# Two narrow half-steps of the last query tile moved from places 12 and 13 to places 7 and 8, with three smaller moves beside them

## The reference, cut to what matters

```
std_attn = softmax(where(mask, -inf, q @ k.T * scale));  std_out = std_attn @ v
geo_attn = softmax(where(mask, -inf, lines_r @ J lines_w.T * inc));  geo_out = geo_attn @ geo_v
y = layernorm(x + ((1-gate)*std_out + gate*geo_out) @ out_w + out_b)
out = layernorm(y + (silu(y @ wg.T) * (y @ wu.T)) @ wd.T)
```

## Time and profile before

| what | value |
|---|---|
| median of 3 runs (lowest, highest) | 1618.38 us (1617.12, 1618.8) |
| the profiled execution's own time | 1618.34 us |
| its span, first to last instruction | 1616.6 us |
| mean granted TensorE clock | 0.985 |
| TensorE matmul busy | 1582.2 us, 98% |
| ScalarE busy | 1199.7 us, 74% |
| VectorE busy | 1055.6 us, 65% |
| GpSimd busy | 341.2 us, 21% |

### The profile page before, as it was taken

How to read it: one execution, slowest core, us unless ns; L and a number is a source line. 1 busy time by engine, 2 the same in 40 slices (tenths; PEclk the granted TensorE clock), 3 DMA queues, 4 the chain that set the end, 5 groups by cost and what they waited for, 6 DMA issues and landing times.

```text
span 1616.6 us, 32075 instructions
## 1 busy us (share of the span) xinstructions
PE 1582.2 (98%) x11809; PEld 579.6 (36%) x11809; DVE 1055.6 (65%) x2584; ACT 1199.7 (74%) x1412; POOL 341.2 (21%) x525
## 2 busy tenths in 40 slices
PE   8999699999999999999999999999999999999998
PEld 5555122222222222222222222222222226666665
DVE  5888977767767676776777767776776514444433
ACT  3444179999999999999999999999999982222212
POOL 5444312211212212021211202111120252321000
PEclk9999589999999999999999999999999999999999
DMA  6889442312122021221312122121204024222000
GB/s 185 245 253 269 139 119 73 95 63 91 48 68 96 24 88 47 68 64 54 107 39 83 43 68 73 45 93 44 73 26 142 21 73 144 90 79 78 26 14 26
DMA packets 103616, 140.39 MB, mean 87 GB/s; under 512 B 14128, under 2 KB 72816, under 8 KB 101392
## 3 DMA queue, kind: packets, MB, share of 16 engines
q1 hardware_dynamic: 102188, 135.10, 26.8%
q0 software_dynamic: 624, 2.75, 0.6%
q10 hardware_dynamic: 628, 0.29, 0.1%
HBM read 81.96 MB, written 55.61 MB: 85 GB/s over the span
## 4 chain that ended last, share of the span: by engine, by line
PE 85%; issue 5%; DVE 5%; ACT 4%; DMA 1%; POOL 0%; SPq 0%; DVEq 0%; POOLq 0%; ACTq 0%
PE pv L1241 30%; PE ex L1147 16%; PE ex L1644 10%; PE ex L1141 7%; PE mx L1181 7%; ACT prob L1330 4%; PE mx L680 3%; PE ex L701 3%; PE mx L1658 2%; PE pv L1658 2%; DVE dull L1356 2%; PE mx L414 1%; DVE mp L1359 1%; PE mx L1664 1%; PE pv L691 1%
## 5 line engine op out<-in xcount | busy, mean ns | idle before, releaser
L1330 ACT ACTIVATE prob<-ex 128x1024 f32<-128x1024 f32 (+1 forms) x1152 | 1056.7, 975 | 95.5 <-PE ex L1147 46.5
L1359 DVE TENSOR_REDUCE mp<-mx 128x1 f32<-128x512 f32 x768 | 492.9, 685 | 192.1 <-PE mx L1181 191.4
L1241 PE MATMUL pv<-prob,va 128*32 128x512 f32 (+3 forms) x5120 | 588.3, 540 | 5.2 <-DVE on L1429 3.0
L1104 POOL TENSOR_SCALAR_AFFINE_SELECT prob<-prob 128x256 f32<-128x256 f32 (+1 forms) x384 | 185.1, 482 | 911.1 <-ACT prob L1330 910.9
L1147 PE MATMUL ex<-dq,dk 64*128 64x512 bf16 (+7 forms) x2560 | 338.2, 350 | 0.4 <-ACT prob L1330 0.4
L1356 DVE CUSTOM_DVE_ANT_0 dull<-mx,mask_qk 128x128 f32<-128x128 f32 (+3 forms) x512 | 223.2, 487 | 74.4 <-PE mx L1181 74.1
L1147 PEld LDWEIGHTS ex<-dq,dk 64*128 64x128 bf16 (+1 forms) x2560 | 78.6, 94 | 431.7 <-ACT prob L1330 423.1
L1181 PE MATMUL mx<-dk,dq 64*128 64x512 bf16 (+3 forms) x1280 | 226.4, 355 | 4.0 <-DVE mp L1356 3.3
L1141 PE MATMUL ex<-gq,gk 38*128 38x512 bf16 (+3 forms) x1280 | 216.0, 349 | 3.2 <-ACT prob L1330 0.9
L1733 ACT ACTIVATE sg<-ex 128x512 f32<-128x512 f32 x48 | 28.7, 597 | 203.5 <-PE ex L1644 203.4
L1241 PEld LDWEIGHTS pv<-prob,va 128*32 128x32 f32 x5120 | 108.3, 108 | 167.1 <-issue 141.5
(11 more groups left out here) (130 smaller groups left out, 948.0 us busy)
## 6 DMA issues: line engine op xcount, KB each, us to landing
values<-vn SPq DMA_DIRECT2D x32, 512.0 KB, 3.8
va<-values SPq DMA_DIRECT2D x16, 1024.0 KB, 4.8
raw<-on SPq DMA_DIRECT2D x64, 256.0 KB
parts_dot<-sp SPq DMA_DIRECT2D x32, 384.0 KB, 4.6
dq<-parts_dot SPq DMA_DIRECT2D x192, 64.0 KB, 3.0
dk<-parts_dot SPq DMA_DIRECT2D x192, 64.0 KB, 2.9
parts_geo<-sp SPq DMA_DIRECT2D x16, 288.0 KB, 3.7
gq<-parts_geo SPq DMA_DIRECT2D x192, 24.0 KB
```

The costliest lines, as they stand in the source:

```text
L1104: g.affine_select(out=cut, in_=cut, compare_op=ALU.is_ge, fill=0.0, base=0, pattern=[[0, nb], [1, P]], channel_multiplier=-1).then_inc(mas ...
L1241: last = pe.matmul(pv[blk * VW:(blk + 1) * VW, CH - w:CH], sets[which]["v"][:, kb, blk * VW:(blk + 1) * VW], prob[UNIT_AT[s, j, kind] % NP ...
L1330: act.activation(prob[n % NPROB][:, :].rearrange("p (b c) -> p b c", b=2)[:, :, 0:w], ex[:, n % 2, :].rearrange("p (b c) -> p b c", b=2)[: ...
L1359: return v.tensor_reduce(out=to, in_=source, axis=AX.X, op=ALU.max)
```

## The change

It puts the narrow places of the fourth query tile at places 7 and 8 (h = 28, 29), moves the 24 geo loads of item 0 ahead of two stores in SyncE's queue, makes GpSimd's `third_part` of chunk 6's geo rows wait for both line writes of chunk 7, and puts `take` between the two reductions of its place.

```diff
-NARROW_AT = ((1, 2), (4, 5), (8, 9), (12, 13))
+NARROW_AT = ((1, 2), (4, 5), (8, 9), (7, 8))
@@ sync, end of project
+            for i in range(LOADS, 2 * LOADS):
+                load(i)
             for m in range(4, NR):
                 store_row(NC - 2, m)
-            for i in range(LOADS, 2 * LOADS):
-                load(i)
@@ gpsimd, project
                     if c == NC - 2 and m == 4:
-                        g.wait_ge(dve, (NC - 1) * LINKS + 5)
+                        g.wait_ge(ln_ready, NC * LN_WRITES)
                     third_part(c, m)
@@ vector, attend: max_tiles_of(it, h) with its loop over a is now max_tile_of(it, h, a)
-                        if h < LEAD or nxt:
-                            if MAX_IN[h]:
-                                max_tiles_of(it, h)
-                            if h in TURN:
-                                turn(it, TURN.index(h))
+                        has_max = (h < LEAD or nxt) and MAX_IN[h]
+                        if has_max:
+                            max_tile_of(it, h, 0)
                         if h == PV_AT[LAST_OF[NQT - 1], 0] + BEHIND - NPV and not head:
                             take(it - 1, NQT - 1, False)
                         for qt in range(NQT - 1):
                             if h == PV_AT[LAST_OF[qt], 0] + BEHIND:
                                 take(it, qt, head)
+                        if has_max:
+                            max_tile_of(it, h, 1)
+                        if (h < LEAD or nxt) and h in TURN:
+                            turn(it, TURN.index(h))
@@ vector, prologue
                 if MAX_IN[h]:
-                    max_tiles_of(-1, h)
+                    for a in range(2):
+                        max_tile_of(-1, h, a)
```

More of the change, by code:

```diff
@@ L1359, in row_max, with max_tile_of @@
                 return v.tensor_reduce(out=to, in_=source, axis=AX.X, op=ALU.max)
[L1361 to L1374, removed]
+            def max_tile_of(it, h, a):
+                i = RING.place[h, a]
+                v.wait_ge(mx_ready, RING.ready(it, i))
+                at = 0
+                for u in MAX_IN[h]:
+                    qb, k0, w, on_diagonal = MAXT[u]
+                    if on_diagonal and not at:
+                        v.sem_inc(v_passed, 1)
+                    last = row_max(mx[:, RING.bank(it, i), at:at + w], mp[DOT][:, a, qb, k0 // CH:k0 // CH + 1], w,
+                                   on_diagonal, dull[:, RING.bank(it, i), at:at + w])
+                    at += w
+                last.then_inc(mx_free, 1)
             def wide_pair(nit, part, n, u):
```

## The result

The changed kernel takes 1620.59 us (median of 20 runs, 1618.86 to 1623.32), the kernel before, run beside it, 1618.23 us (20 runs, 1616.54 to 1619.40). The ratio is 1.0015 with an interval of [1.0009, 1.0021]: 2.4 us longer. That is within the 0.2% that the prediction called no change that can be told, although the interval leaves out 1: a slowdown of this size, of the sign that was forecast, stands in these runs. The forecast was 1620.0, the range 1613.5 to 1624.5. The profiled execution has 1620.58 us and a span of 1618.8.

The account below looks back on a forecast made before the run. The prediction took TensorE's order inside an item to bound the kernel, with 85% of the chain of waits. Terms -6.3 - 4.1 + 0.3 + 9.4 + 2.4 = +1.7 us on 1618.34 gave 1620.0, range 1613.5 to 1624.5.

Parts of the forecast that it names:

- narrow places, 15 items: TensorE, items 0 to 14: h = 27 to next h = 1 takes 19.16 instead of 19.58 us; -6.3 us in all.
- copy at h = 11, 15 items: VectorE copies after only the first reduction, so the next value products start 0.28 us earlier; -4.1 us in all.
- hold and loads: Chunks 6 and 7: VectorE gains 1.56 us from GpSimd's hold, but late stores take it back; +0.3 us.
- the wait in the last item: TensorE waits for h = 28's mask behind GpSimd's third weighing, itself waiting for chunk 2's loads; +9.4 us.
- low clock after it: After the last item's gap TensorE restarts at half clock for some 6 us; +2.4 us, bounds 0 and +5.
- four wide periods, h = 32 to 0, 7.92: Term of the narrow-places sum: TensorE's four wide periods after the turn take 7.92 us.
- the whole item repeats like this for h = 22 to 35: TensorE's steady items before the change: wide places at 1.98 us each, repeating through that stretch.
- Rival (b): Last item's stall is absent or absorbed; faster, sum -10.1 us, 1608.2 us; chance 0.12.
- Rival (c): Narrow places do nothing where they now are, the rest stands; 1626.3 us; chance 0.06.
- rival (a): Low clock stays after the last item's gap and stores come late; slower, 1622.6 us with +5 of clock; chance 0.26.

Follow-up runs that it names:

- e5: Changed kernel with the last item's third weighing moved between GpSimd's masks of h = 29 and h = 35; 1608.11 us, ratio 0.9943.
- e9: Changed kernel with 21 idle matmuls in TensorE's gap of the last item; 1619.32 us, ratio 1.0006.
- e8: Kernel before with GpSimd's hold alone, the 24 loads left behind the two geo stores; 1620.01 us, ratio 1.0011.
- e4: Changed kernel with the last item's third weighing moved behind GpSimd's last mask; 1611.59 us, ratio 0.9961.
- e1: Kernel before with the narrow places moved alone; 1624.43 us, ratio 1.0035.
- e7: Changed kernel with the narrow places at 5 and 6 (h = 26, 27) instead of 7 and 8; 1631.16 us, ratio 1.0081.
- e3: Kernel before with GpSimd's hold and the new order of the loads together; 1618.48 us, ratio 0.9997.
- e11: Kernel before with the 24 loads ahead of the two stores alone, GpSimd's hold as it was; 1618.3 us, ratio 1.0004.
- e6: Changed kernel with 35 idle matmuls in TensorE's gap of the last item; 1624.78 us, ratio 1.0042.

## Why the prediction was right

The time came out 0.6 us from the forecast, and by the mechanisms named. That it came so close is partly luck: against the table below, four of the five terms of the forecast are off by +1.0, -0.3, +0.5 and -0.8 us, and these errors nearly cancel. The parts, measured on the traces of before and after unless an experiment is named:

| step | predicted | measured |
|---|---|---|
| narrow places, 15 items | -6.3 | -0.35 x 15 = -5.3 |
| copy at h = 11, 15 items | -4.1 | -0.27 x 15 = -4.1 |
| hold and loads | +0.3 | 0.0 |
| the wait in the last item | +9.4 | 11.54 - 1.6 = +9.9 (e5, e9) |
| low clock after it | +2.4 | +1.6 (e9) |
| item 0 beyond its share | none | -1.0 |
| chunk 7 starts later | none | +1.0 |
| sum | +1.7 | +2.1, with the span +2.2 |

- **Narrow places.** Right in kind: the sequence h = 6 to 11 did give the later one. The term that was mis-sized is "four wide periods, h = 32 to 0, 7.92": the last of them, at h = 35, is 2.06. The geo scores of h = 0 start 0.30 after the tile of maxima where other places have 0.22 (717.39 to 717.61 is one such pair in the same trace). That they have further waits, for the new item's operands and maxima, which used to be covered, is my reading of the code and was not tested. The prediction also read the old order too evenly: "the whole item repeats like this for h = 22 to 35" is not so in before, where the turn's place takes 2.33 and the places from h = 32 on are shorter than 1.98. Its sum used measured stretches and does not rest on that sentence.
- **Copy.** Right in size and place.
- **Hold and loads.** The net was right, and its kind: the hold wins, and the stores take it back. The win is larger than the 1.56 put, though: 2.2 us up to the rests of rows, since the squares are faster too, of which 1.46 are left at row (7, 5) in e8. And the prediction took the loads' move as mere cost, while e8 shows that without it the first exponential comes 1.8 us later than in before (51.35 against 49.53).
- **The wait.** Right, and the largest term. It is 0.5 longer than put. The steps behind the weighing came as put: from the mask to the products 0.82 us against 0.84, from the products to the dot scores of h = 35 10.54 (e5) against 10.6. But the weighing starts 21.5 us after the end of the copy of h = 22 instead of 20.7. In the traces with the old narrow places this distance is 20.1 to 21.5 us, in those with new ones 21.1 to 21.9 (e4, which moves the weighing, left out), so it partly belongs to the execution; why it is longer with the new places is open. e5 confirms the cause: the same places, only the weighing elsewhere in GpSimd's order, and 11.54 us come back.
- **Clock.** Right in kind and 0.8 too dear: I expected the low clock for some 6 us of work, and it was 4.1. The price for each of them, 3.4 / 9 = 0.38 us, held: 4.1 x 0.38 = 1.6. The 4.1 is one draw; in e1 the low clock behind the gap lasted 3.6 us, in e7 5.0.
- **Not in the forecast.** Two rows of the table, which cancel here by chance. In item 0 the low clock ended 5.8 us after the first exponential, in before 8.4, which gives back 1.0; in the eleven experiments, with and without each edit, it is 5.2 to 6.4, so the 8.4 of before is the odd one and no edit's doing. And chunk 7's first product is 0.98 late before any changed instruction has run. In the 13 traces that instant is 157.1 to 157.7 us after the start where the granted clock first rose at 10.8 to 12.2, and 156.3 to 156.8 where it rose at 9.3 to 10.3. That this too is the execution's is likely and not shown: with one trace for each kernel, all four without the loads ahead are in the early group and seven of the nine with them in the late one, while the medians of e3 and e11 are within 0.6 us of before's.

Rival (b) put the kernel without the stall at 1608.2. That is a kernel one can build, and e5 measures it at 1608.11. To a tenth this is luck, since the measured parts give -5.3 - 4.1 + 0.0 = -9.4 and not -10.1; the interval of e5's ratio is 2 us to either side. Rival (c) falls with e1, and rival (a) with the clock's 1.6 us and the hold's 0.0.

## What to carry to other kernels

When masks or any due work moves earlier on an engine that serves its list in order, look at what else stands in that list ahead of it: here a weighing, invisible before, became a wait of 10 us once, as dear as 0.6 us won in 15 items. Move the waiting step to the last slot where it is still in time rather than simply out of the way, since late work meets new neighbours (e4 lost 2.1 us so). And a change that nets to nothing is worth taking apart: two of its four parts were good, and one line elsewhere releases them.

## What the runs showed that I had not expected

- GpSimd's clears stretch VectorE's small casts tenfold, 0.18 to 1.89 and 1.82 us (e8), and its weighing stretches four normalisations from 1.38 to 3.48 us (e4). A reduction of 0.25 us (line 1393) beside the first of those clears was not touched.
- A gap of 9.88 us on TensorE cost only 1.6 us of clock afterwards. The Trainium skill (TensorE: Matmul & The Clock Gate, "What's actually happening") describes the lowered rate as the engine's state at rest; e9, where idle matmuls keep it at work, shows a granted clock of 1.00 throughout, and by that rule nothing should then be lost: the 12.84 us of e9 and e5 agree.
- A float32 matmul of 128 output rows and 256 columns takes 0.44 us by itself (e6), while four value matmuls of 32 output rows and 512 columns take 1.06 together. A filler has to be priced by its own form.
